# A normalised state turned by DMA transposes in f16 halves instead of by fp32 TensorE transposes

## What is computed

```
x = x + tanh(g_xattn[0]) * L0_xattn(layernorm(x), ctx)      # one softmax over 77 context rows
x = x + tanh(g_ffn[0])   * L0_ffn(layernorm(x))             # ternary linear, gelu, ternary linear, with RMS norms
x = x + tanh(g_xattn[1]) * L1_xattn(layernorm(x), ctx)      # 16 heads of 32, softmax over 77 context rows
x = x + tanh(g_ffn[1])   * L1_ffn(layernorm(x))             # silu-gated, inputs and weights fake-quantised to fp4
```

## Time and profile before

| | us |
|---|---|
| median of 3 runs | 1964.47 |
| lowest, highest | 1952.07, 1965.97 |
| the profiled execution | 1966.61 |
| span of the profiled execution | 1964.8 |

### The profile page before, as it was taken

How to read it: one execution, slowest core, us unless ns; L and a number is a source line. 1 busy time by engine, 2 the same in 40 slices (tenths; PEclk the granted TensorE clock), 3 DMA queues, 4 the chain that set the end, 5 groups by cost and what they waited for, 6 DMA issues and landing times.

```text
span 1964.8 us, 24465 instructions
## 1 busy us (share of the span) xinstructions
PE 1389.0 (71%) x8184; PEld 709.4 (36%) x8184; DVE 1591.1 (81%) x2429; ACT 679.0 (35%) x1977; POOL 427.6 (22%) x309
## 2 busy tenths in 40 slices
PE   4145436769786797679776978778767986697654
PEld 3121113424362345334442436234533453243321
DVE  6989997886877787868788788778787888787796
ACT  3113104541273316341454126421734154314310
POOL 1109400071004400260016100440026002510000
PEclk8567767989998899889998999889988999799887
DMA  9262340001200110001000120011000200001002
GB/s 337 107 192 65 97 129 31 1 11 22 59 9 11 22 43 24 9 14 52 26 6 7 21 66 2 11 22 43 24 12 11 54 23 6 17 24 31 7 16 53
DMA packets 135208, 84.42 MB, mean 43 GB/s; under 512 B 102650, under 2 KB 119546, under 8 KB 132502
## 3 DMA queue, kind: packets, MB, share of 16 engines
q1 hardware_dynamic: 135062, 82.61, 15.0%
HBM read 49.04 MB, written 8.39 MB: 29 GB/s over the span
## 4 chain that ended last, share of the span: by engine, by line
issue 44%; DVE 36%; PE 14%; ACT 2%; POOL 2%; DMA 1%; POOLq 0%; DVEq 0%; ACTq 0%; SPq 0%
PE bank L1052 12%; DVE amax L789 4%; DVE pair L798 4%; DVE hid L794 3%; PE bank L1147 2%; DVE pair L806 2%; DVE th L842 2%; DVE pair L808 1%; DVE ex L743 1%; DVE pair L819 1%; ACT region L493 1%; DMA hqt<-pair 1%; DVE hid L846 1%; DVE xb L794 1%; DVE pair L813 1%
## 5 line engine op out<-in xcount | busy, mean ns | idle before, releaser
L1052 PE MATMUL bank<-xt,w_up 128*128 128x512 f16 x1024 | 261.9, 407 | 62.9 <-ACT region L451 47.5
L1052 PE MATMUL bank<-w_gate,xqt 128*128 128x512 bf16 x512 | 152.7, 427 | 204.0 <-DVE th L842 159.3
L1147 PE MATMUL bank<-w_dn,region 128*128 128x512 fp8e4 x1024 | 235.1, 385 | 41.3 <-issue 34.8
L466 ACT ACTIVATE th<-bank,half_cg 128x512 f32<-128x512 f32 x128 | 87.9, 686 | 487.0 <-PE bank L1052 487.0
L381 POOL TENSOR_TENSOR region<-g,region 128x512 f16<-128x512 f32 x128 | 178.0, 1393 | 184.0 <-ACT region L451 176.9
L842 DVE SCALAR_TENSOR_TENSOR th<-th,bank 128x512 f32<-128x512 f32 x128 | 87.5, 683 | 148.6 <-ACT th L466 148.6
L385 POOL TENSOR_TENSOR acc<-acc,sq 128x512 f32<-128x512 f32 x120 | 195.8, 1632 | 0.0
L1052 PEld LDWEIGHTS bank<-xt,w_up 128*128 128x128 fp8e4 x1024 | 104.9, 105 | 213.0 <-issue 121.0
L493 ACT ACTIVATE region<-bank,nm 128x77 f32<-128x77 f32 x512 | 160.8, 349 | 54.1 <-DVE nm L888 54.1
L1052 PE MATMUL bank<-w_down,hqt 128*128 128x512 bf16 x512 | 131.0, 414 | 59.7 <-DMA hqt<-pair 59.7
L1147 PEld LDWEIGHTS bank<-w_dn,region 128*128 128x128 f16 x1024 | 101.2, 100 | 165.7 <-issue 50.5
(11 more groups left out here) (209 smaller groups left out, 2713.1 us busy)
## 6 DMA issues: line engine op xcount, KB each, us to landing
xin<-in_x SPq DMA_DIRECT2D x16, 512.0 KB, 3.9
out_x<-x SPq DMA_DIRECT2D x16, 512.0 KB, 2.8
region<-in_w_up_t SPq DMA_DIRECT2D x1, 4096.0 KB, 13.3
hid<-in_gate_w SPq DMA_DIRECT2D x4, 1024.0 KB, 4.7
x<-in_gate_w SPq DMA_DIRECT2D x4, 1024.0 KB, 4.8
hid<-in_up_w SPq DMA_DIRECT2D x4, 1024.0 KB, 4.8
x<-in_up_w SPq DMA_DIRECT2D x4, 1024.0 KB, 4.8
hid<-in_down_w SPq DMA_DIRECT2D x4, 1024.0 KB, 5.9
```

Of the source, the lines that this page charges most:

```text
L466: eng.activation(th[:, u % 2, :], bank[4][:, :], ACT.Tanh, scale=half_cg[:, :]).then_inc(sg["th"], 1)
L1052: last = mm(out, lhs, rhs, start=(n == 0), stop=(n == len(pairs) - 1))
L1147: last = mm(bank[2 + t % 2][:, :], ht[i][:, f, t * P:(t + 1) * P], w_dn[:, f, :], start=(f == 0 and i == 0), stop=(f == KF - 1 and i == 1))
```

## The change

The state is split before it is turned, and the turning is done by DMA, two row tiles at a time. The index a is 0 for tiles 0 and 1, and 1 for tiles 2 and 3.

- `xn` shrinks to two row tiles. `norm(stage, g, src, 0)` writes tiles 0 and 1; `norm(stage, g, src, 1)` waits until the subtraction of the first half is done and writes tiles 2 and 3 into the same place. Stage 2: steps 17 and 18. Stage 3: slots 33 and 34. Stage 1: slots 37 and 39.
- ACT copies `xn` (128x1024, SBUF) to `xs[0]` in f16: two per stage. The one of stage 2 stands at steps 17 and 18, ahead of what `attend` has in the same step; those of stage 1 stand at slots 37 and 39, between and behind the copies of `query(2)` and `query(3)`.
- POOL subtracts, `xs[1] = xn - xs[0]` (128x1024): two per stage, those of stage 2 ahead of `root4(g3, 0)`, those of stage 3 and 1 behind their `root`.
- SP issues four DMA transposes per stage (`turn_state`: high and low half, a = 0 and 1), 12 per group, each of 256 KB. In the loop the ones of stage 2 stand ahead of `turn_x`, those of stage 3 behind `load_x`, those of stage 1 behind `turn_h(g, 3)` and a wait for all four query products, ahead of `store(g, 1)`.
- PE loses the 48 transposes per group and waits for the DMAs instead; `up` and `query` read `xt`, now laid out by row tile, in the same number of matmuls.
- `p3` moves to the place of `q32` in `region`.

```diff
@@
-        xt = [sb(f"xt{i}", [P, KD, T], F16) for i in range(2)]
+        xt = [sb(f"xt{i}", [P, TILES, KD, P], F16) for i in range(2)]
...
-        xn = f32_at(half, TILES * D).rearrange("p (t d) -> p t d", t=TILES)
-        at = half + 2 * TILES * D
-        p3 = f32_at(at, 2 * HC * M).rearrange("p (r h m) -> p r h m", r=2, h=HC)
+        p3 = f32_at(2 * KD * T, 2 * HC * M).rearrange("p (r h m) -> p r h m", r=2, h=HC)
+        xn = f32_at(half, 2 * D).rearrange("p (t d) -> p t d", t=2)
+        xs = [region[:, half + (i + 1) * TILES * D:half + (i + 2) * TILES * D].rearrange("p (t d) -> p t d", t=TILES)
+              for i in range(2)]
@@ sync
+            def turn_state(stage, g, a):
+                ts = slice(2 * a, 2 * a + 2)
+                for i, made in enumerate((f"xh{stage}", f"xl{stage}")):
+                    want(sp, made, g, a + 1)
+                    sp.sem_inc(sm["sp_passed"])
+                    sp.dma_start_transpose(xt[i][:, ts].rearrange("p t k c -> p (t k) c"),
+                                           xs[i][:, ts].rearrange("p t d -> p (t d)")).then_inc(sg[f"xt{stage}{'ab'[a]}"], 16)
...
+            def turns(g, g1, g2):
+                if g1 is not None:
+                    for a in range(2):
+                        turn_state(2, g1, a)
                 for h in range(2):
                     turn_x(g, h)
                 turn_h(g, 0)
                 turn_h(g, 1)
                 store(g, 0)
                 turn_h(g, 2)
+                if g2 is not None:
+                    want(sp, "x2", g1)
+                    load_x(g2)
                 if g1 is not None:
-                    want(sp, "x2", g1 - 1)
-                    load_x(g1)
+                    for a in range(2):
+                        turn_state(3, g1, a)
                 turn_h(g, 3)
+                if g2 is not None:
+                    want(sp, "qp", g1)
+                    sp.sem_inc(sm["sp_passed"])
+                    for a in range(2):
+                        turn_state(1, g2, a)
                 store(g, 1)
@@ gpsimd
+            def x_lo(stage, g, a):
+                ts = slice(2 * a, 2 * a + 2)
+                want(pool, f"xh{stage}", g, a + 1)
+                eng.tensor_tensor(xs[1][:, ts], xn[:, :, :], xs[0][:, ts], ALU.subtract).then_inc(sg[f"xl{stage}"], 1)
+
             def phase_a(g3, g1):
                 if g1 is not None:
                     want(pool, "var2", g1)
                     eng.tensor_tensor(sdev[:, :, :], ve2[:, :, :], powers[:, :, :], ALU.pow).then_inc(sg["rstd2"], 1)
+                    for a in range(2):
+                        x_lo(2, g1, a)
                 if g3 is not None:
                     root4(g3, 0)
...
                 root(3, g)
+                for a in range(2):
+                    x_lo(3, g, a)
                 if g1 is not None:
                     root(1, g1)
+                    for a in range(2):
+                        x_lo(1, g1, a)
@@ scalar
-            def x_hi(stage, g, t):
-                want(act, f"tr{stage}", g, t + 1)
-                eng.activation(xt[0][:, :, t * P:(t + 1) * P],
-                               bank[t % 2][:, :].rearrange("p (k t) -> p k t", k=KD),
-                               ACT.Copy).then_inc(sg[f"xh{stage}"], 1)
+            def x_hi(stage, g, a):
+                ts = slice(2 * a, 2 * a + 2)
+                want(act, f"xn{stage}", g, 2 * a + 2)
+                eng.activation(xs[0][:, ts], xn[:, :, :], ACT.Copy).then_inc(sg[f"xh{stage}"], 1)
...
-                for t in T2_AT.get(n - 1, ()):
-                    x_hi(2, g, t)
+                if n in (NORM2_AT, NORM2_AT + 1):
+                    x_hi(2, g, n - NORM2_AT)
...
                     if s == SLOT_T3:
-                        for t in range(TILES):
-                            x_hi(3, g, t)
+                        for a in range(2):
+                            x_hi(3, g, a)
                     if SLOT_Q <= s < SLOT_Q + NC:
                         query(g, s - SLOT_Q)
+                    if g1 is not None and s == SLOT_NORM1:
+                        x_hi(1, g1, 0)
+                    if g1 is not None and s == SLOTS - 1:
+                        x_hi(1, g1, 1)
@@ vector
+                if a:
+                    want(dve, f"xl{stage}", g, 1)
+                for t in (2 * a, 2 * a + 1):
+                    eng.tensor_scalar(xn[:, t % 2, :], src[:, t, :], mv[:, 0, t, 0:1], scale[:, t:t + 1],
                                       ALU.subtract, ALU.mult).then_inc(sg[f"xn{stage}"], 1)
-            def x_lo(stage, g, t):
-                want(dve, f"xh{stage}", g, t + 1)
-                sl = slice(t * P, (t + 1) * P)
-                eng.tensor_tensor(xt[1][:, :, sl], bank[t % 2][:, :].rearrange("p (k t) -> p k t", k=KD),
-                                  xt[0][:, :, sl], ALU.subtract).then_inc(sg[f"xl{stage}"], 1)
...
-                    if s == SLOT_NORM3:
-                        norm(3, g, xb)
-                    if s == SLOT_T3:
-                        for t in range(TILES):
-                            x_lo(3, g, t)
+                    if s in (SLOT_NORM3, SLOT_T3):
+                        norm(3, g, xb, s - SLOT_NORM3)
...
                     if s == SLOT_NORM1 and g1 is not None:
                         norm1(g1)
+                    if s == SLOTS - 1 and g1 is not None:
+                        norm(1, g1, xin, 1)
@@ tensor
-                if (u := tile1_at(n, 0)) is not None:
-                    x_t(1, g, u)
-                for t in T2_AT.get(n, ()):
-                    x_t(2, g, t)
                 if n in UP_AT:
                     up(g, UP_AT[n])
 
             def up(g, f):
                 if f < 2:
-                    want(pe, "xl2", g)
+                    want_state(2, g, 0)
+                    pe.sem_inc(sm["pe_passed"])
+                    want_state(2, g, 2)
...
                         if s == SLOT_Q:
-                            want(pe, "xl3", g)
+                            want_state(3, g, 0)
+                            pe.sem_inc(sm["pe_passed"])
+                            want_state(3, g, 2)
                         query(g, s - SLOT_Q)
```

101 lines of the change are left out of this document (48 added, 53 removed).

## The result

| | before | after |
|---|---|---|
| median, 4 runs each | 1964.38 us | 2021.41 us |
| lowest, highest | 1952.07, 1965.97 | 2020.06, 2023.13 |
| span of the profiled execution | 1964.8 | 2021.3 |
| mean granted TensorE clock over the span | 0.877 | 0.839 |

The changed kernel takes 1.0305 times as long, 95% interval 1.0262 to 1.0347: slower by 3.1%, where 2.2% (2008 us, at most 2040) had been forecast. The engine totals first (part 1 of the page; the row of before is in the earlier trace rows).

The account below looks back on a forecast made before the run. No engine bounds every stage; new serial chains count. First phase with state 2 18.9, handover 16.2, group 0 and preamble 8, last group 1: 44 us on the median 1964.47, so 2008 us, 2.2% slower; 8-in-10 range 1966 to 2040.

Parts of the forecast that it names:

- the signs that the prediction named: Turn 216 to 218 us, up(0) 2.5 us or more later by DMA, lower clock there, DVE idle for POOL, table load.
- The waits are hidden: Rival: no real change, all four terms at their cheap ends, 8 us more, 1972 us; chance 0.16.
- DVE is the bound: Rival: freed DVE work shortens attention's last steps and quant4 to phase_b's end, 32 us won, 1932 us; chance 0.13.
- The loop's handover: State 1 of the next group, slots 37 to 39: first exponential 2.7 us later per turn, six turns, 16.2 us.
- The gain of the first phase: Attention steps with stage1: work removed from PE, DVE and ACT gains 1.5 us per group, ends 0 and 2.7.
- State 2: Steps 17 to 20: up(0) 2.7 us later, plus 1.5 for PE's clock; 4.2 us per group, ends 2.2 and 6.5.
- The term of 1.5 us per group for the lower clock: In state 2: after some 5 us idle, PE runs up(0) at 1.2 GHz, adding 1.5 us per group.
- State 3: Slots 33 to 36: quant4 starts 0.9 us earlier; query(0) starts 4 us later, covered by quant4; no cost.
- covered as well: In state 3: queries starting at the lower clock add 1.5 us, which costs nothing.
- Group 0: Its handover has no quant4 or out4: state lands 5 to 6 us late, state 1's chain behind it; 7 us.
- the preamble: Group 0's preamble: DVE waits 3.5 us twice and loses eight subtractions of 0.68; 1 us more.
- POOL against DVE: Rival: POOL's 48 more subtractions each hold DVE, or are held, 1 us on the path: 2056 us; chance 0.11.

Follow-up runs that it names:

- all moves: Changed kernel with state 1's first copy behind query(3), its second half in the next phase, own second-half place (states 2, 3), state 2's norms and copies reordered: 1973.14 us.
- the filler: Changed kernel with matmuls on PE that nothing reads, 22 ahead of the queries and 16 ahead of attend(2): 2009.76 us, 1.0214.
- state 3 alone: Kernel before with only state 3 split and turned by DMA, states 1 and 2 still turned by TensorE: 1973.21 us, 1.0030.
- the two with all moves and fillers: The best order found plus 22 unread matmuls per group ahead of the queries: 1964.54 us; the same with 10 more at step 19: 1967.89 us.
- the best order found: All moves, plus in the preamble the first block maximum ahead of state 1's second half, third weight piece's load between the halves' transposes: 1968.81 us.

## Why the prediction was right, and where its steps were off

The sign, the size to 13 us, and the mechanism hold: serial chains took the place of parallel work in stages that their engines did not bound. The sum was less good than it looks, since terms off in both directions cancelled: state 2 was priced 13 us too high and the gain of the first phase 13 us too high as well, and what remains is the handover, group 0 and the preamble, all too small.

Of the signs that the prediction named, two came as it said: the turn of the loop at 216 to 218 us, and the first exponential right behind a table load. Three came in part. `up(0)` is released by the DMA, but 2.2 us later and not 2.5 or more. The lower clock fell on it in three groups of seven. And DVE has idle time released by POOL before the second half of state 3 only (1.74 us in the turn shown); before those of states 1 and 2 other work of DVE fills that wait, but for once in the preamble (3.3 us each).

- **The rivals that ended lower.** "The waits are hidden" (1972) and "DVE is the bound" (1932) both fell: DVE lost 46 us of work and no stretch shrank by anything like it. The busy share of 81% was an average over stages, as the prediction said. (The 1972 is also mis-added: it subtracts 1.8 us per group for the first phase, where the term's own end is 2.7; with that it is 1966. Nothing hangs on it.)
- **The loop's handover (16.2 forecast, 20.1 measured).** The mechanism was right, and the experiment that moved the first half's copy and the whole second half shows it: with them gone, the stretch is as before. The term was too small by 0.6 us per turn, and the part that was mis-sized is ACT's idle time at the loop's end. Up to the end of ACT's second copy the turn ran as forecast (6.84 us behind norm 1; forecast 6.7 to 7.1). Then ACT spends 3.10 us on nothing that the profile shows, not 1.68; in the five turns with this idle time it was 1.8 to 3.1, 2.4 in the mean. Ahead of the first and behind the last turn of the loop ACT has none, and there too the stretch grew by 3.5 and 3.4 us, from 4.7 to 8.2. So the loop's end is not what the change added: DVE's 2.31 us stood in the path before, ACT's stand in it now, and the rest is the longer chain. `ql(3)` takes 1.55 us beside POOL's subtraction, where 0.69 is usual. By the Trainium skill (SBUF — State Buffer, "Who interferes with whom") a DVE operation with two SBUF inputs contends with a GpSimd instruction that reads SBUF, and the ports that they share are an exclusive lock. The trace agrees: POOL's subtraction began at 774.14 and ended at 776.26, `ql(3)` began at 775.25 and ended at 776.80, half a microsecond behind it. The wait is what is left of the other's instruction, here 0.9 us, not the whole 2.12. On the path it counts for 0.5 us, since the second half had to wait for POOL until 776.26 anyway, and the prediction had allowed for it.
- **The gain of the first phase (1.5 per group forecast, 0.4 lost).** This step failed. It priced work taken from PE, ACT and DVE in the stage where PE is nearly full as time won, at PE's unchanged rate. PE's share bought nothing on balance: with the transposes back the time is the same. What the runs show in its place is a lower clock in that stage, 0.88 in the turn shown and not 0.96: PE's first matmuls ran at 1.2 GHz until 790.2, 7 us into the stage, and again from 800.5 to 804.2; in the kernel before only for its first 5 us. With all moves made, the phase is 0.85 us shorter per group (5.9 in seven) at a clock of 0.96. So there was a gain, of half the size, and only behind the repair of other steps. Why the clock was lower stays open. PE had been idle for 5.5 us before the stage's first matmuls, but in the kernel with all moves it is idle for 4.9 to 5.5 us at the same place in the turns of the loop.
- **State 2 (4.2 per group forecast, 2.3 measured).** The start of `up(0)` came 2.0 us late, not 2.7; the copy, the subtraction and the DMA were each a little cheaper than priced. The reason was only half seen. The prediction had the second half wait for POOL, and had ACT's copy slip `attend`'s copies by some 3 us, "still inside the same wait". The runs show that the slip makes a wait as long as POOL's: with POOL's taken away the stretch stayed at 11.42, with ACT's order changed as well it fell to 9.96. The term of 1.5 us per group for the lower clock was too large. In four groups the lower clock fell on `w_o` of tile 2 alone (5.28 and not 2.75 us in the turn shown), where it lay inside the wait for the DMA. In the other three it reached `up(0)` too and cost 1.4 to 1.7 us there, as forecast: 4.7 us in seven groups and not 10.5, of which 2.9 were won back ahead of `down`.
- **State 3 (nothing forecast).** `quant4` starts its maximum at 751.42, 5.3 us behind norm 3 and not 6.5, a gain of 1.2 where 0.9 was forecast. But "covered as well" was wrong for the queries' clock: 13.20 us and not 10.52 after 6.77 us of idle time eats the 1.2 us, and the filler, with the queries at 10.53, gives them back. The cover was counted at PE; the queries' reader, `ql` on DVE ahead of norm 1, had none.
- **Group 0 (7 forecast, 9.7) and the preamble (1 forecast, 7.8).** The first is a term a little too small: 6.2 us for the later state, where 5 to 6 were forecast, and 3.5 for state 1's chain. In the second two things were overlooked. One is PE's side of group 0's own state 2, of which the sum had DVE's wait alone: norm 2 to `up(0)` is 1.9 us longer there too. The other, 5.8 us up to norm 2, is in part SP's queue. The prediction counted DVE's waits there and not what is queued behind `turn_state(1, 0)` on SP, the weight pieces, the next of which was asked for 7.5 us later; undoing this order brings norm 3 of group 0 from 5.2 to 2.5 us behind the kernel before, and the median down by 4.3.
- **POOL against DVE (2056).** As a cost on the path it is there only at `ql(3)`: 0.5 us in each of seven groups, so by the rows some 3 us in all and not 48. Where the second half of norm 3 no longer waits for POOL it runs beside its subtraction and takes 2.53 us instead of 1.00, so that wait and contention trade places.

What stays open: whether all turns could be brought under 211 us for good. Gains in one stretch are often followed by a stretch in which PE runs the same work at its lower clock; the runs show this in three kernels (state 3 alone, and the two with all moves and fillers), but not a rule for when it happens. Whether the kernel before would gain from fillers of its own was not tried either. That the 0.6 us per group left in state 2 come from the serial length of the new chain (half a norm 1.0, a copy 1.1, two subtractions 4.2, a transpose 2.8 to 3.6 us, against 9.4 in all before) is argued from the rows, not tried. Group 0 supports it: with no `attend` beside the chain it has 9.95 to 9.99 us in every kernel whose second half has a place of its own, whatever the order.

## What to carry to other kernels

Moving work to idle engines and to DMA makes it cheaper in engine time and longer in a chain; look at who reads the result next, and at every instruction queued behind the new one, on every queue. Here, 53 of the 57 us came from order and a shared buffer (a copy ahead of others on ACT, a transpose ahead of loads on SP, half of a state that waits for the other's place), not from the transposes' price. Yet the best order found stays 3 us behind the kernel before (1968.8 against 1965.8 us), and with fillers it only equals it (1964.5 against 1965.1). When PE is made to wait, price the clock of what it does next, and follow who waits for that.

## What the runs showed of the hardware

- A DMA transpose of 256 KB (128x1024 f16) lands 2.8 us after issue, in sets of four on one queue; ACT copies 128x1024 fp32 to f16 inside SBUF in 1.06 us, POOL subtracts it in 2.12.
- ACT's idle time at the loop's end was 1.7 us in each turn of the kernel before, where ACT arrived early and the time vanished into a wait, and 1.8 to 3.1 us in the changed kernel, where it arrived late and the time stood in the path.
- A table load of ACT takes 1.28 us, and where no loop's end lies at it the work on both sides follows within 0.02 us.
- PE's lower clock falls on whatever comes behind the idle time, and moving work moves it: `w_o` at 1.2 GHz and `up(0)` at 2.4 in one kernel, the reverse in the next (5.30 and 1.89 us, then 2.76 and 3.52). Holding the clock with matmuls that nothing reads was worth 12 us in the changed kernel (22 and 16 in each group) and 3 to 4 in the one with all moves (22, hardly clear of the noise); 10 more in the wrong place cost some 3.
